# A graph-recurrent layer in three stages: one memory map, and three groups of loads and set-up work moved ahead of their stage

## The chip, the core and the metric

One core of a Trainium2 chip runs the whole program. The metric is device microseconds from one launch, and the kernel before and the kernel after are timed on the same kind of chip. The engines are named as in the profile: PE (matmul) with its weight loads PEld, DVE, ACT, POOL, and SP, which issues DMAs.

## The reference

The input is 2048 samples of 50 nodes with 32 features, the number of maskers is 2. In short:

```
adj  = relu(x.reshape(B, 1600) @ masker_param[t] + masker_bias[t])      # B x 2 x 50 x 50
adj  = adj / (adj.sum(-1) + 1e-6)
m    = adj @ (x @ weight)                                               # B x 2 x 50 x 32
gates = m @ w_ih.T + b_ih + x @ w_hh.T + b_hh ;  r, z, n                # a GRU cell
h    = (1 - z) * tanh(r * n) + z * x
h    = batchnorm over B (3200 features), then layernorm per sample
w    = softmax over nodes of (h @ attn_w + attn_b);  out = sum_n w * h  # B x 64
```

The batch statistics need h of all samples, so the last part can't start before the whole of h is there.

## The kernel before

The batch is cut into 16 tiles of 128 samples. Three stages follow each other, each in a block of its own: all engines leave a block together before any enters the next.

**Stage 1** (`stage1`, L84) makes the normalised adjacency and stores it in HBM (`adjT`). The 5000 columns are 10 groups of 500, the tiles two blocks of 8; for each block and group, eight windows, one for each tile, of 38 matmuls (L340), 160 windows in all. Both operands are split into a high and a low part by ACT and DVE (`split_x_hi`, `split_x_lo`, `split_w_hi`, `split_w_lo`). In the window that follows, ACT applies the relu (L229), DVE normalises (L276 to L284), PE transposes (L321), ACT evacuates (L235), and SP stores (L138). SP waits at the end for its last stores (L171, L172).

**Stage 2** (`stage2`, L379) first loads four small weight arrays (L455), multiplies two of them (L663), lets DVE lay the product and `whh` out in the blocks of `wd` (24 copies, L559 and L560), and splits `wd` (L471 on ACT, L565 on DVE). Then it goes through the tiles in 8 rounds each, with two buffers for the tile's data: `adj_sb` in two DMAs from `adjT` (L440), `xs_sb` (L442) and `xg_sb` (L445). A round s on PE is `aggregate(s + 1)` (L674) and then `gates(s)` (L699, L705). In round 6 of a tile the PE waits, between these two, for the next tile's `adj` and `xs` (`adj_loaded`, in `gates`). ACT splits `xg` in four parts (L486), POOL makes the low part (L652). With h of a tile ready, DVE turns it (L614), PE transposes it in seven batches of up to four chunks through one PSUM bank (L716, `turn_chunks`), ACT copies each (L498) and stores it (L505) and DVE takes statistics (L603). For the last tile these seven batches run after the rounds, with nothing beside them.

**Stage 3** (`stage3`, L737) loads 12 arrays (L839) and then h of its first block of 512 samples in 28 DMAs (L848, seven sets of three or four chunks). DVE forms mean and variance (L879 to L888), waits for all 12 arrays, and goes on from L891 to the coefficients `Csq` (L904). ACT waits for the same arrays, casts the `spread` matrix (L1035, read from the second half of `h3`, so `load_h(1)` waits for this cast), loads its table and takes the square root (L1037). With `Csq`, ACT squares the 25 chunks of a block (L1047 for PE, L1052 for POOL); POOL adds 14 of them in 13 steps (L1134), PE closes the sums (L1177), and the softmax and the pooling of the block follow. All queues are in order and the order is written out by hand; semaphores tie the engines.

Of the kernel before, what the change touches and what calls it, by code (L numbers as in the profile page):

```python
# [10 lines left out]

# [4 lines left out]
fp32 = mybir.dt.float32  # L16
# [67 lines left out]
def stage1(nc, psum, xT, W, adjT, ident_d):  # L84
    with ExitStack() as ctx:
        sb = lambda name, shape, dt=fp32: ctx.enter_context(nc.sbuf_tensor(name, shape, dt))
        sem = lambda name: ctx.enter_context(nc.semaphore(name))
        x_hi = sb("x_hi", [P, KC, BLK * P], fp32r)
        x_lo = sb("x_lo", [P, KC, BLK * P], fp32r)
# [3 lines left out]
        w_raw = sb("w_raw", [P, KC + 1, GW])  # L93
# [4 lines left out]
        at = sb("at", [RK, 2, AK, P])  # L98

# [6 lines left out]
        at_stored = [sem("at_stored0"), sem("at_stored1")]  # L106
        dve_step = sem("dve_step")

# [11 lines left out]
        def _(sp):  # L120
# [25 lines left out]
            sp.dma_start(ident[:, :], ident_d).then_inc(ident_loaded, 16)  # L146
            for blk in range(BLOCKS):
                for it, group in p1_iters(sp, blk):
                    for w in range(BLK):
# [17 lines left out]
                        if isinstance(it, int) and it == GROUPS - 1 and blk + 1 < BLOCKS:  # L167
                            load_x(BLK + w, 0)
                            load_x(BLK + w, 1)
            store_tile(ITERS * BLK - 1, 1, TILES - 1, GROUPS - 1)  # L170
            sp.wait_ge(at_stored[0], 16 * (ITERS * BLK // 2))  # L171
            sp.wait_ge(at_stored[1], 16 * (ITERS * BLK // 2))  # L172

        def split_x_hi(act, bt, half):
            act.wait_ge(x_loaded[half], 16 * (bt + 1))
            if bt >= BLK and half == 0:

                act.wait_ge(mm_done, (GROUPS - 1) * BLK + bt - BLK + 1)
            cols = bass.ts(bt % BLK, P)
            if half == 0:  # L180
                nc.scalar.copy(x_hi[:, 0:XH, cols], x_raw[:, 0:XH, :]).then_inc(x_hi_ready, 1)
            else:
                nc.scalar.copy(x_hi[:, XH:KF, cols], x_raw[:, XH:KF, :])
                nc.scalar.copy(x_hi[0:KLAST, KF, cols], x_raw[0:KLAST, KC, :])
                nc.scalar.copy(x_lo[:, KF, cols], x_raw[:, KF, :]).then_inc(x_hi_ready, 1)

        def split_x_lo(dve, bt, half):
            dve.wait_ge(x_hi_ready, 2 * bt + half + 1)
            cols = bass.ts(bt % BLK, P)
            k0, k1 = (0, XH) if half == 0 else (XH, KF)  # L190
            last = nc.vector.tensor_tensor(x_lo[:, k0:k1, cols], x_raw[:, k0:k1, :], x_hi[:, k0:k1, cols].bitcast(fp32),
                                           ALU.subtract)
            if half:
                last = nc.vector.tensor_tensor(x_lo[KR:P, KF, cols], x_raw[KR:P, KF, :], x_lo[KR:P, KF, cols].bitcast(fp32),
# [29 lines left out]
        def _(act):  # L224
# [17 lines left out]
            for blk in range(BLOCKS):  # L242
                for it, group in p1_iters(act, blk):
                    static = isinstance(it, int)
                    for w in range(BLK):
# [18 lines left out]
                        if static and it == GROUPS - 1 and w >= 1:  # L264
                            for half in range(2):
                                split_x_hi(act, BLK + w - 1, half)
            c = ITERS * BLK - 1
# [4 lines left out]
        def _(dve):  # L272
            def normalise(c, c2, start=False):
# [8 lines left out]
                if not start:  # L282
                    dve.wait_ge(tr_done, c - 1)
                nc.vector.tensor_tensor(an[:, c2], u[:, c2], rows[:, 2].unsqueeze(2).to_broadcast([P, GN, N]),  # L284
                                        ALU.mult).then_inc(an_ready, 1)

# [5 lines left out]
            for blk in range(BLOCKS):  # L292
                for it, group in p1_iters(dve, blk):
                    static = isinstance(it, int)
                    for w in range(BLK):
# [12 lines left out]
                        if static and it == GROUPS - 1 and w >= 1:  # L308
                            for half in range(2):
                                split_x_lo(dve, BLK + w - 1, half)  # L310
            normalise(ITERS * BLK - 1, 1)

        @block.tensor
        def _(pe):
# [9 lines left out]
            def window(it, w, blk, c, start=False, bank_free=False, none_before=False):  # L324
# [3 lines left out]
                cols = bass.ts(w, P)  # L328
                for i, (k0, k1) in enumerate(UNITS):
# [4 lines left out]
                    for k in range(k0, k1):  # L334
# [4 lines left out]
                        for n, (a, b, r) in enumerate(products):  # L339
                            last = nc.tensor.matmul(mm_out(w % 2), a[0:r, k, cols], b[0:r, k, :],  # L340
# [10 lines left out]
            for blk in range(BLOCKS):  # L351
                for it, group in pe_iters(pe, blk):
# [26 lines left out]
def stage2(nc, psum, ins, adjT, hF, stats):  # L379


    with ExitStack() as ctx:
        sb = lambda name, shape, dt=fp32: ctx.enter_context(nc.sbuf_tensor(name, shape, dt))
        sem = lambda name: ctx.enter_context(nc.semaphore(name))
        adj = sb("adj_sb", [2 * N, 2, TN, SH])
        xs = sb("xs_sb", [2 * N, 2, SH, 2 * D])
        xg = sb("xg_sb", [P, 2, ROUNDS, N * QB])
# [4 lines left out]
        hC = sb("hC", [P, FC, P])  # L392
        ident = sb("ident2_sb", [P, P])
        m_hi = sb("m_hi", [P, 2, RC], fp32r)
        m_lo = sb("m_lo", [P, 2, RC], fp32r)
        r_gate = sb("r_gate", [P, RC])
        n_in = sb("n_in", [P, 2, RC])
        wT4 = sb("wT4_sb", [D, P])
        wih = sb("wih_sb", [D, 3 * D])
        whh4 = sb("whh_sb", [P, 3 * D])  # L400
        biases = sb("biases_sb", [P, 2, 3])
        bias = sb("bias", [P, 3])
        wd = sb("wd", [P, 2, 2, P])
        wd_hi = sb("wd_hi", [P, 2, 2, P], fp32r)
        wd_lo = sb("wd_lo", [P, 2, 2, P], fp32r)

        consts_loaded, ident_loaded = sem("consts_loaded"), sem("ident_loaded")
        g_product, zeroed, blocks_ready = sem("g_product"), sem("zeroed"), sem("blocks_ready")
        wd_hi_ready, wd_ready, bias_ready = sem("wd_hi_ready"), sem("wd_ready"), sem("bias_ready")
        adj_loaded = [sem("adj_loaded0"), sem("adj_loaded1")]  # L410
        xg_loaded = [sem("xg_loaded0"), sem("xg_loaded1")]
# [19 lines left out]
        turn_bank = psum[:, 7 * BANK:8 * BANK]  # L431
# [5 lines left out]
        def _(sp):  # L437
            def load_adj(tile, r):
                for half in range(2):
                    sp.dma_start(adj[N * half:N * half + N, r], adjT[tile, :, SH * half:SH * half + SH].rearrange("(c m) s -> m c s", m=N)  # L440
                                 ).then_inc(adj_loaded[r], 16)
                sp.dma_start(xs[:, r], ins["xz"][tile]).then_inc(adj_loaded[r], 16)  # L442

            def load_xg(tile, r):
# [911 lines left out]
```

## Time and profile before

| what | us |
|---|---|
| median of 3 runs (2312.24 to 2316.13) | 2314.57 |
| the profiled execution's own time | 2318.24 |
| its span | 2316.5 |
| stage 1, to the last copy of the adjacency (L235) | 1463.95 |
| from there to the first aggregation of stage 2 (L674) | 38.9 |
| stage 2, to the last store of h issued (L505) | 2080.84 |
| from there to the first square of stage 3 (L1052) | 27.7 |
| mean granted clock of PE over the span, of full speed | 0.973 |

The profile is of one execution; times in it count from the start of its span. PE is busy for 2198.9 us of it (95%), DVE for 47%, ACT for 42%, POOL for 6%. Matmuls are pipelined, so a busy PE is not a PE at its peak.

### The profile page before, as it was taken

How to read it: one execution, taken by the hardware profiler on the slowest of the kernel's cores; microseconds unless marked ns; L12 is line 12 of the kernel's file. 1: busy time of each engine (PE TensorE's matmuls, PEld its weight loads, DVE VectorE, ACT ScalarE, POOL GpSimd, SP SyncE). 2: the span in 40 equal slices, each digit the busy share in tenths (PEclk: the TensorE clock that was granted, in tenths of full speed). 3: DMA queues.
4: the chain of work that ended last, by engine and by line, in shares of the span. 5: the costliest groups of instructions: out<-in, count | busy, mean ns of one | idle time of the engine just before them, and what ended most of it. 6: DMA issues, size and time to landing. Idle time of an engine off the chain costs nothing. (4 is left out here: it accounts for less than half of the span.)

```text
span 2316.5 us, 34741 instructions
## 1 busy us (share of the span) xinstructions
PE 2198.9 (95%) x12302; PEld 1737.8 (75%) x12302; DVE 1091.0 (47%) x2177; ACT 962.2 (42%) x1637; POOL 136.2 (6%) x124
## 2 busy tenths in 40 slices
PE   8999999999999999999999999299999999975888
PEld 7888888888888888888888888277777777752333
DVE  4433233332345223333233332178888888873656
ACT  4322122221234212222122221088888988865551
POOL 0000000000000000000000000011101111104340
PEclk9999999999999999999999999699999999986899
DMA  6421222212234222221222211577777677619440
GB/s 208 151 75 44 88 91 90 74 45 88 92 128 143 64 90 90 91 69 50 89 90 91 72 48 27 124 171 184 186 201 181 188 199 181 181 65 261 122 119 5
DMA packets 341744, 264.06 MB, mean 114 GB/s; under 512 B 169334, under 2 KB 302998, under 8 KB 339990
## 3 DMA queue, kind: packets, MB, share of 16 engines
q1 hardware_dynamic: 323546, 225.69, 34.5%
q10 hardware_dynamic: 18144, 37.69, 5.0%
q8 instruction: 29, 0.48, 0.1%
q14 instruction: 25, 0.20, 0.0%
HBM read 195.65 MB, written 67.70 MB: 114 GB/s over the span
## 5 line engine op out<-in xcount | busy, mean ns | idle before, releaser
L340 PE MATMUL psum<-w_hi,x_lo 128*128 128x500 f32 x2080 | 823.0, 396 | 8.6 <-DVE w_lo L216 8.6
L340 PE MATMUL psum<-w_lo,x_hi 128*128 128x500 f32 (+1 forms) x2080 | 811.0, 390 | 0.0
L340 PE MATMUL psum<-w_hi,x_hi 128*128 128x500 f32 x1920 | 745.1, 388 | 0.0
L276 DVE TENSOR_REDUCE rows<-u 128x10 f32<-128x500 f32 x160 | 107.7, 673 | 893.5 <-ACT u L229 892.8
L340 PEld LDWEIGHTS psum<-w_hi,x_lo 128*128 128x128 f32 x2080 | 392.1, 188 | 84.4 <-issue 7.9
L340 PEld LDWEIGHTS psum<-w_lo,x_hi 128*128 128x128 f32 (+1 forms) x2080 | 392.5, 189 | 73.2
L340 PEld LDWEIGHTS psum<-w_hi,x_hi 128*128 128x128 f32 x1920 | 361.7, 188 | 72.9
L235 ACT COPY at<-psum 125x512 f32<-125x512 f32 x160 | 93.8, 586 | 677.4 <-PE psum L321 677.4
L229 ACT ACTIVATE u<-psum 128x500 f32<-128x500 f32 x160 | 94.1, 588 | 342.4 <-PE psum L340 342.3
L674 PE MATMUL psum<-adj_sb,xs_sb 100*64 100x100 f32 x2048 | 200.6, 350 | 30.1 <-DMA xs_sb<-xz 30.1
L674 PEld LDWEIGHTS psum<-adj_sb,xs_sb 100*64 100x64 f32 x2048 | 144.4, 149 | 73.9 <-issue 63.7
L652 POOL TENSOR_TENSOR xg_lo<-xg_sb,xg_hi 128x400 fp32r<-128x400 f32 x64 | 67.1, 1049 | 1961.4 <-ACT xg_hi L486 1961.4
L520 ACT ACTIVATE r_gate<-psum,bias 64x400 f32<-64x400 f32 x256 | 151.2, 591 | 18.3 <-PE psum L699 15.8
L216 DVE TENSOR_TENSOR w_lo<-w_raw,w_hi 128x1000 fp32r<-128x1000 f32 x120 | 144.1, 1201 | 23.6 <-ACT w_hi L210 17.4
L210 ACT CAST w_hi<-w_raw 128x1000 fp32r<-128x1000 f32 (+1 forms) x140 | 135.6, 969 | 46.3 <-PE psum L340 45.0
L525 ACT ACTIVATE psum<-psum,bias 64x400 f32<-64x400 f32 x256 | 142.3, 556 | 12.7 <-DVE hG L595 6.9
L284 DVE TENSOR_TENSOR an<-u,rows 128x500 f32<-128x500 f32 x160 | 108.8, 680 | 6.9
L603 DVE BATCH_NORM_STATS2 stats<-hC 128x128 f32 (+1 forms) x400 | 88.7, 282 | 49.3 <-ACT hC L498 48.9
L321 PEld LDWEIGHTS psum<-ident_sb,an 128*125 128x125 f32 x640 | 94.1, 186 | 17.8 <-DVE an L284 3.2
L321 PE MATMUL psum<-ident_sb,an 128*125 128x128 f32 x640 | 96.0, 272 | 4.0 <-DVE an L284 4.0
L1013 DVE SCALAR_TENSOR_TENSOR pr<-h,nmu_sb,psum 128x512 f32<-128x512 f32 x100 | 70.5, 743 | 47.0 <-PE psum L1221 24.6
L570 DVE TENSOR_TENSOR m_lo<-psum,m_hi 128x400 fp32r<-128x400 f32 x128 | 70.6, 552 | 28.6 <-ACT m_hi L490 28.6
(160 smaller groups left out, 2284.8 us busy)
## 6 DMA issues: line engine op xcount, KB each, us to landing
w_raw<-W SPq DMA_DIRECT2D x140, 500.0 KB, 7.9
adjT<-at SPq DMA_DIRECT2D x160, 250.0 KB
adj_sb<-adjT SPq DMA_DIRECT2D x32, 1250.0 KB
xs_sb<-xz SPq DMA_DIRECT2D x16, 1600.0 KB
hF<-hC ACTq DMA_DIRECT2D x96, 256.0 KB, 6.7
h<-hF SPq DMA_DIRECT2D x64, 256.0 KB, 4.5
xg_sb<-xg ACTq DMA_DIRECT2D x14, 800.0 KB, 8.0
h<-hF SPq DMA_DIRECT2D x48, 192.0 KB, 3.7
```

Of the source, the lines that this page charges most:

```text
L210: nc.scalar.copy(w_hi[:, k0:k1, :], w_raw[:, k0:k1, :]).then_inc(w_hi_ready, 1)
L216: nc.vector.tensor_tensor(w_lo[:, k0:k1, :], w_raw[:, k0:k1, :], w_hi[:, k0:k1, :].bitcast(fp32), ALU.subtract).then_inc(w_ready, 1)
L229: nc.scalar.activation(u[:, c2].rearrange("p n m -> p (n m)"), mm_out(c2), ACT.Relu).then_inc(u_ready, 1)
L235: nc.scalar.copy(at[:, c2].rearrange("p k b -> p (k b)"), tr_out(c2)).then_inc(at_ready, 1)
L276: nc.vector.tensor_reduce(rows[:, 0], u[:, c2], AX.X, ALU.add).then_inc(dve_step, 1)
L284: nc.vector.tensor_tensor(an[:, c2], u[:, c2], rows[:, 2].unsqueeze(2).to_broadcast([P, GN, N]), ALU.mult).then_inc(an_ready, 1)
L321: last = nc.tensor.transpose(tr_out(c2)[:, k * P:(k + 1) * P], flat[:, k * RK:(k + 1) * RK], ident[:, :])
L340: last = nc.tensor.matmul(mm_out(w % 2), a[0:r, k, cols], b[0:r, k, :], start=k == 0 and n == 0, stop=k == KF and n == 1)
L520: last = nc.scalar.activation(r_gate[half], rz_bank(pair)[half], ACT.Sigmoid, bias=bias[half, R_G:R_G + 1])
L525: last = nc.scalar.activation(z_bank[half], rz_bank(pair)[other], ACT.Sigmoid, bias=bias[other, Z_G:Z_G + 1])
L603: last = nc.vector.bn_stats(stats[:, bass.ds(tile, 1), c, :].rearrange("p i v -> p (i v)"), hC[:, c, :])
L674: last = nc.tensor.matmul(out_[SH * i:SH * i + SH, :, gi], xs[:, r, b, :], adj[:, r, :, b], start=True, stop=True)
```

## The change

All of SBUF becomes one allocation, and every buffer gets a fixed place in it (`place`, `Bump`), and some buffers of a later stage share their place with buffers that the stage before has finished with. `x_hi` and `x_lo` are laid out tile by tile instead of chunk by chunk. Semaphores and buffers that two stages use are made once (`Shared`).

- In stage 1 SP loads the four small weight arrays right after its first loads; PE makes their product between the two blocks; in the last group DVE lays out `wd` (third window), ACT casts it (fourth), DVE splits it (fifth). SP loads `adj`, `xs` and `xg` of tile 0 in the last group, over `w_raw`, the first tiles of `x_hi` and of `x_lo`. The waits for the last stores move from the end of stage 1 into stage 2, behind the loads of tile 1.
- In stage 2 SP loads nine of the 12 arrays of stage 3 after the loads of tile 3, and five of the seven sets of h of the first block once tile 14's aggregations are through. The last tile's transposes alternate between two PSUM banks.
- In stage 3 `ident` is that of stage 2; SP loads the last two sets of h first, then `spread` and `pool_mask`. DVE waits for those two only before `pool_cols`. ACT loads the square root's table with a one-element activation at the start, squares two sets, and then waits for the two arrays and casts `spread`.
- h in `h3` is stored by sets (`PLACE_OF`), so that a set is one contiguous stretch.

```diff
+AT_H = 600
+AT_W_RAW, AT_X_HI = 0, (KC + 1) * GW
+AT_X_LO = AT_X_HI + BLK * KC * P
+AT_XG = AT_X_LO + 4 * KC * P
+AT_WEIGHTS = 51616
+AT_EARLY = 47768
...
+XS_TILES, XG_TILES = 3, 5
...
+def load_adj(sp, shared, adjT, tile, r=0):
+    for half in range(2):
+        sp.dma_start(shared.adj[r][N * half:N * half + N], adjT[tile, :, SH * half:SH * half + SH].rearrange("(c m) s -> m c s", m=N)
+                     ).then_inc(shared.adj_loaded[r], 16)
+def load_xs(sp, shared, ins, tile, r=0):
+    sp.dma_start(shared.xs[r][:], ins["xz"][tile]).then_inc(shared.adj_loaded[r], 16)
...
+        w_raw = place("w_raw", [P, KC + 1, GW], AT_W_RAW)
+        x_hi = place("x_hi", [P, BLK, KC, P], AT_X_HI, fp32r)
+        x_lo = place("x_lo", [P, BLK, KC, P], AT_X_LO, fp32r)
...
+            for dst, src in ((shared.wT4, "wT4"), (shared.wih, "wihT"), (shared.whh4, "whhT4"), (shared.biases, "biases")):
+                sp.dma_start(dst[:], ins[src]).then_inc(shared.weights_loaded, 16)
...
+                        if isinstance(it, int) and it == ITERS - 1:
+                            if w == 0:
+                                sp.wait_ge(w_ready, ITERS * NU)
+                                for c2 in range(2):
+                                    sp.wait_ge(at_stored[c2], 16 * (GROUPS * BLK // 2))
+                                load_adj(sp, shared, adjT, 0)
+                            if w == XS_TILES:
+                                sp.wait_ge(mm_done, it * BLK + XS_TILES)
+                                load_xs(sp, shared, ins, 0)
+                            if w == XG_TILES:
+                                sp.wait_ge(mm_done, it * BLK + XG_TILES)
+                                load_xg(sp, shared, ins, 0)
             store_tile(ITERS * BLK - 1, 1, TILES - 1, GROUPS - 1)
-            sp.wait_ge(at_stored[0], 16 * (ITERS * BLK // 2))
-            sp.wait_ge(at_stored[1], 16 * (ITERS * BLK // 2))
...
-                nc.scalar.copy(x_hi[:, 0:XH, cols], x_raw[:, 0:XH, :]).then_inc(x_hi_ready, 1)
+                nc.scalar.copy(x_hi[:, w, 0:XH, :], x_raw[:, 0:XH, :]).then_inc(x_hi_ready, 1)
...
+            def weight_blocks(dve):
+                wd = shared.wd
+                dve.wait_ge(w_ready, ITERS * NU)
+                nc.vector.memset(wd[:], 0.0).then_inc(zeroed, 1)
+                dve.wait_ge(zeroed, 1)
+                dve.wait_ge(shared.weights_loaded, 64)
+                dve.wait_ge(g_product, 1)
+                for j in range(4):
+                    q = slice(D * j, D * j + D)
+                    pair, one = divmod(j, 2)
...
+                        nc.vector.tensor_copy(wd[q, 0, of, first:first + D], g_bank[q, e])
+                        last = nc.vector.tensor_copy(wd[q, 1, of, first:first + D], shared.whh4[q, e])
+                last.then_inc(blocks_ready, 1)
+                nc.vector.tensor_tensor(shared.bias[:], shared.biases[:, 0], shared.biases[:, 1], ALU.add).then_inc(shared.bias_ready, 1)
...
+                        if static and it == ITERS - 1 and w == 2:
+                            weight_blocks(dve)
+                        if static and it == ITERS - 1 and w == 4:
+                            dve.wait_ge(wd_hi_ready, 1)
+                            nc.vector.tensor_tensor(shared.wd_lo[:], shared.wd[:], shared.wd_hi[:].bitcast(fp32),
+                                                    ALU.subtract).then_inc(shared.wd_ready, 1)
...
+                if blk == 1:
+                    pe.wait_ge(shared.weights_loaded, 64)
+                    nc.tensor.matmul(g_bank, shared.wT4[:], shared.wih[:], start=True, stop=True).then_inc(g_product, 1)
...
+SETS = [(n, list(range(n, FC, QC))) for n in range(QC)]
+SET_AT = [sum(len(cs) for _, cs in SETS[:n]) for n in range(QC)]
+PLACE_OF = {c: SET_AT[n] + j for n, cs in SETS for j, c in enumerate(cs)}
+EARLY_SETS = 5
+A_SLOT = TN * SH + SH * 2 * D
+assert EARLY_SETS < QC and SET_AT[EARLY_SETS] * CW <= A_SLOT
+def load_set(sp, shared, hF, i, n):
+    at = slice(SET_AT[n], SET_AT[n] + len(SETS[n][1]))
+    for k in range(CB):
+        sp.dma_start(shared.h[:, i % 2, at, k * P:(k + 1) * P], hF[i * CB + k, :, slice(n, FC, QC), :]).then_inc(shared.h_loaded[i % 2][n], 16)
...
-        turn_bank = psum[:, 7 * BANK:8 * BANK]
...
+        def turn_bank(tile, n):
+            bank = 0 if isinstance(tile, int) and tile == TILES - 1 and n % 2 else 7
+            return psum[:, bank * BANK:(bank + 1) * BANK]
...
+                        load_adj(sp, shared, adjT, tile + 2, r)
+                        load_xs(sp, shared, ins, tile + 2, r)
             sp.dma_start(ident[:], ins["ident"]).then_inc(ident_loaded, 16)
-            load_xg(1, 1)
-            load_adj(1, 1)
+            load_xg(sp, shared, ins, 1, 1)
+            load_adj(sp, shared, adjT, 1, 1)
+            load_xs(sp, shared, ins, 1, 1)
+            for c2 in range(2):
+                sp.wait_ge(shared.at_stored[c2], 16 * (ITERS * BLK // 2))
             iteration(0, True)
+            for dst, src in early_loads(shared, ins):
+                sp.dma_start(dst, src).then_inc(shared.early_loaded, 16)
             with sp.Fori(1, TILES // 2 - 1) as it:
                 iteration(it, True)
-            iteration(TILES // 2 - 1, False)
+            sp.wait_ge(ax_done, (TILES - 1) * ROUNDS)
+            for n in range(len(batches)):
+                sp.wait_ge(hC_stored[n], 16 * CB)
+            for n in range(EARLY_SETS):
+                load_set(sp, shared, hF, 0, n)
...
+                wait(pe, hC_ready, tile * len(batches) + (n - 1 if isinstance(tile, int) and tile == TILES - 1 and n else n))
...
+def early_loads(shared, ins):
+    return [(shared.quarter[:], ins["quarter"]), (shared.score_mask[:], ins["score_mask"]),
+            (shared.square_mask[:], ins["square_mask"]), (shared.fold_out[:], ins["fold_out"]), (shared.par[:], ins["par"]),
+            (shared.aw[:], ins["aw"]), (shared.ab[:], ins["attn_b"].partition_broadcast(P)),
+            (shared.rowpar[:], ins["rowpar"]), (shared.t_mask[:], ins["t_mask"])]
...
-        loads = [(ident[:], ins["ident"]), (quarter[:], ins["quarter"]),
-                 (score_mask[:], ins["score_mask"]), (square_mask[:], ins["square_mask"]),
-                 (pool_mask[:], ins["pool_mask"]), (spread_raw, ins["spread"]), (fold_out[:], ins["fold_out"]),
-                 (par[:], ins["par"]), (aw[:], ins["aw"]), (ab[:], ins["attn_b"].partition_broadcast(P)),
-                 (rowpar[:], ins["rowpar"]), (t_mask[:], ins["t_mask"])]
+        loads = [(spread_raw, ins["spread"]), (pool_mask[:], ins["pool_mask"])]
         @block.sync
         def _(sp):
-            for dst, src in loads:
...
+            def load_h(i, first=0):
+                for n in range(first, QC):
...
+                        sp.wait_ge(pr_ready, FC * (i - 2) + 1 + max(order.index(c) for c in SETS[n][1]))
+                    load_set(sp, shared, hF, i, n)
...
-            load_h(0)
+            load_h(0, EARLY_SETS)
+            for dst, src in loads:
+                sp.dma_start(dst, src).then_inc(loaded, 16)
...
-            dve.wait_ge(loaded, 16 * len(loads))
+            dve.wait_ge(shared.early_loaded, 16 * len(early_loads(shared, ins)))
...
+            dve.wait_ge(loaded, 16 * len(loads))
...
-            act.wait_ge(loaded, 16 * len(loads))
-            nc.scalar.copy(spread[:].rearrange("p c f -> p (c f)"), spread_raw).then_inc(spread_ready, 1)
+            act.wait_ge(step_done, 2)
+            nc.scalar.activation(warm[:], eps[:], ACT.Sqrt)
...
-            squares(0, *range(QC))
+            squares(0, 0, 1)
+            act.wait_ge(loaded, 16 * len(loads))
+            nc.scalar.copy(spread[:].rearrange("p c f -> p (c f)"), spread_raw).then_inc(spread_ready, 1)
+            squares(0, *range(2, QC))
```

## Rows read from the trace of the kernel before

**Rows 1.** Busy tenths of PE in 40 slices of 57.9 us, from the page

```profile
PE   8999999999999999999999999299999999975888
```

**Rows 2.** Timeline around the first boundary: start, us, engine, line, operation, idle before

```profile
1459.66 0.39 PE L340 MATMUL psum<-w_lo,x_hi 97*128 97x500 f32 x1
...
1460.72 0.67 DVE L276 TENSOR_REDUCE rows<-u 128x10 f32<-128x500 f32 x1 [7.19 <-ACT u L229]
...
1463.36 0.59 ACT L235 COPY at<-psum 125x512 f32<-125x512 f32 x1 [2.67 <-PE psum L321]
1468.84 0.36 SPq L455 DMA_DIRECT2D wT_sb<-wT  x1
...
1471.12 10.27 SPq L440 DMA_DIRECT2D adj_sb<-adjT  x2
...
1471.97 0.74 PE L663 MATMUL psum<-wih_sb,wT_sb 32*128 32x96 f32 x2 [8.65 <-DMA biases_sb<-biases]
...
1490.60 21.07 SPq L440 DMA_DIRECT2D adj_sb<-adjT  x2
...
1502.84 2.98 PE L674 MATMUL psum<-adj_sb,xs_sb 100*64 100x100 f32 x32 [30.13 <-DMA xs_sb<-xz]
...
1505.80 0.70 PE L699 MATMUL psum<-m_hi,wd_lo 64*128 64x400 f32 x2
```

**Rows 3.** Timeline of DVE, ACT and SP at the end of the second stage

```profile
2071.46 0.83 DVE L603 BATCH_NORM_STATS2 stats<-hC 128x6 f32<-128x128 f32 x4
...
2071.91 0.59 ACT L498 COPY hC<-psum 128x512 f32<-128x512 f32 x1 [1.27 <-PE psum L716]
...
2080.84 0.34 ACTq L505 DMA_DIRECT2D hF<-hC  x1
...
2082.84 0.37 SPq L839 DMA_DIRECT2D ident_sb<-ident  x1
```

**Rows 4.** Timeline of DVE, ACT, POOL and PE at the head of the third stage

```profile
2089.42 0.99 DVE L888 TENSOR_REDUCE var_sb<-pr 128x25 f32<-128x800 f32 x1
...
2102.04 2.86 ACT L1035 CAST spread_sb<-h 100x3200 fp32r<-100x3200 f32 x1 [21.23 <-DMA t_mask_sb<-t_mask]
2104.91 1.28 ACT L1037 ACT_TABLE_LOAD   x1
...
2106.62 0.32 DVE L896 RECIPROCAL inv_sb<-bnstd_sb 128x25 f32<-128x25 f32 x1 [3.67 <-ACT bnstd_sb L1037]
...
2108.54 1.52 ACT L1052 ACTIVATE sqp<-h,Csq_sb,A_sb 128x512 f32<-128x512 f32 x2 [2.02 <-DVE Csq_sb L904]
...
2120.23 9.78 POOL L1134 TENSOR_TENSOR acc<-acc,sqp 128x512 f32<-128x512 f32 x7 [2.36 <-ACT sqp L1052]
...
2131.97 1.04 PE L1177 MATMUL psum<-acc,square_mask_sb 128*32 128x512 f32 x2 [2.27 <-POOL mark L1137]
```

**Rows 5.** Groups by line: busy us, mean ns, idle before

```profile
L486 ACT CAST xg_hi<-xg_sb 128x400 fp32r<-128x400 f32 x64 | 33.6, 529 | 0.0
...
L559 DVE COPY wd<-psum 32x32 f32<-32x32 f32 x12 | 2.2, 182 | 3.4 <-PE psum L663 3.3
```

**Rows 6.** Timeline of PE around the seventh round of the first tile

```profile
1531.35 0.45 PE L699 MATMUL psum<-m_hi,wd_lo 64*128 64x400 f32 x2
```

**Rows 7.** Stretches: busy time of PE, PEld, DVE, ACT, POOL, granted clock, DMA share, GB/s

```profile
1471.00:1529.00 58.00, 26.90 (x218) 21.47 (x219) 18.36 (x52) 21.69 (x41) 5.64 (x6) 0.68 0.75 175
1529.00:1532.00 3.00, 3.00 (x28) 2.37 (x28) 1.83 (x4) 2.86 (x7) 0.51 (x1) 1.00 0.05 11
2020.00:2040.00 20.00, 20.00 (x174) 15.74 (x174) 16.85 (x39) 17.51 (x35) 2.18 (x3) 1.00 0.09 32
```

**Rows 8.** Waits of the SP queue over the whole span

```profile
SPq L440 <- PE psum L674: 231.0, 14, 17.9
```

**Rows 9.** Stretches at the head of the third stage, columns as in rows 7

```profile
2094.00:2102.00 8.00, 0.00 (x0) 0.00 (x0) 0.00 (x0) 0.00 (x0) 0.00 (x0) 0.50 0.65 143
2104.00:2116.00 12.00, 7.44 (x38) 6.12 (x42) 8.79 (x19) 9.65 (x13) 5.36 (x4) 0.50 1.16 292
```

More of the change, by code:

```diff
@@ L12 @@
+import math
 import concourse.bass as bass
 from concourse import mybir
+from collections import namedtuple
 from contextlib import ExitStack
@@ L266, in _ @@
                                 split_x_hi(act, BLK + w - 1, half)
+                        if static and it == ITERS - 1 and w == 3:
+                            act.wait_ge(blocks_ready, 1)
+                            nc.scalar.copy(shared.wd_hi[:], shared.wd[:]).then_inc(wd_hi_ready, 1)
             c = ITERS * BLK - 1
@@ L285, in normalise @@
                                         ALU.mult).then_inc(an_ready, 1)
+            def weight_blocks(dve):
[8 more added lines that the diff above has]
+                    pair, one = divmod(j, 2)
+                    at = {R_G: SH * pair + D * one, Z_G: SH - SH * pair + D * one, N_G: D * j}
+                    for gate, first in at.items():
+                        of, e = (N_W if gate == N_G else RZ_W), slice(D * gate, D * gate + D)
+                        nc.vector.tensor_copy(wd[q, 0, of, first:first + D], g_bank[q, e])
+                        last = nc.vector.tensor_copy(wd[q, 1, of, first:first + D], shared.whh4[q, e])
+                last.then_inc(blocks_ready, 1)
+                nc.vector.tensor_tensor(shared.bias[:], shared.biases[:, 0], shared.biases[:, 1], ALU.add).then_inc(shared.bias_ready, 1)
             split_x_lo(dve, 0, 0)
@@ L437, in _ @@
         def _(sp):
[L438 to L444, printed above, removed]
-                sp.dma_start(xg[:, r], ins["xg"][tile]).then_inc(xg_loaded[r], 16)
             def iteration(it, more):
@@ L548, in _ @@
         def _(dve):
-            nc.vector.memset(wd[:], 0.0).then_inc(zeroed, 1)
-            dve.wait_ge(zeroed, 1)
-            dve.wait_ge(consts_loaded, 64)
-            dve.wait_ge(g_product, 1)
-            for j in range(4):
-                q = slice(D * j, D * j + D)
-                pair, one = divmod(j, 2)
-                at = {R_G: SH * pair + D * one, Z_G: SH - SH * pair + D * one, N_G: D * j}
-                for gate, first in at.items():
-                    of, e = (N_W if gate == N_G else RZ_W), slice(D * gate, D * gate + D)
-                    nc.vector.tensor_copy(wd[q, 0, of, first:first + D], psum[q, e])
-                    last = nc.vector.tensor_copy(wd[q, 1, of, first:first + D], whh4[q, e])
-            last.then_inc(blocks_ready, 1)
-            nc.vector.tensor_tensor(bias[:], biases[:, 0], biases[:, 1], ALU.add).then_inc(bias_ready, 1)
-            dve.wait_ge(wd_hi_ready, 1)
-            nc.vector.tensor_tensor(wd_lo[:], wd[:], wd_hi[:].bitcast(fp32), ALU.subtract).then_inc(wd_ready, 1)
             dve.wait_ge(bias_ready, 1)
@@ L661, in _ @@
         def _(pe):
-            pe.wait_ge(consts_loaded, 64)
-            nc.tensor.matmul(psum[:, 0:3 * D], wT4[:], wih[:], start=True, stop=True).then_inc(g_product, 1)
             pe.wait_ge(wd_ready, 1)
@@ L673, in aggregate @@
                         b = 32 * i + q * QB + gi
-                        last = nc.tensor.matmul(out_[SH * i:SH * i + SH, :, gi], xs[:, r, b, :], adj[:, r, :, b], start=True, stop=True)
+                        last = nc.tensor.matmul(out_[SH * i:SH * i + SH, :, gi], xs[r][:, b, :], adj[r][:, :, b], start=True, stop=True)
                 last.then_inc(ax_done, 1)
```

170 lines of the change are left out of this document (88 added, 82 removed).

## The prediction

> **What bounds the kernel now.** I read the page's busy line first, then the two places where it dips. PE is at 8 tenths or more from the start to slice 37 of 40, except in slice 26 (2 tenths) and in slices 36 to 40 [rows 1]. So PE sets the time of stages 1 and 2, and stage 3 is a chain over all engines. The change adds no work inside the loops; what it can give back lies at the two dips. The timeline of the first dip: the last matmul of stage 1 starts at 1459.66, the last copy of the adjacency ends at 1463.36 + 0.59 = 1463.95, SP gets to stage 2 only at 1468.84, and PE starts its first aggregation at 1502.84, after 30.13 us of waiting for a DMA [rows 2]. The weight product at 1471.97 and all that DVE does with it is over long before; the loads alone end this wait. The second dip: the last store of h is issued at 2080.84, stage 3 opens at 2082.84 [rows 3], DVE has the variance at 2089.42 + 0.99 = 2090.41, yet ACT gets its arrays only at 2102.04, casts `spread` (2.86), loads a table (1.28), and DVE's reciprocal comes at 2106.62 and the first square at 2108.54 [rows 4]. The last seven batches of transposes before it go at 1.27 + 0.59 = 1.86 us each, PE and ACT taking turns over one bank [rows 3].
>
> **The first boundary.** Loads of tile 0 move into the last group, the wait for the last stores moves behind the loads of tile 1. After 1463.95 remain the issue of one store (0.34 to 0.36 [rows 2, 3]) and the change of blocks. I put that change at 0.8: its bounds are 0 and 2.0, the whole of the way from the last store to the next stage's first DMA at the other boundary, landing included [rows 3]. PE then aggregates from 1465.1 on: 1502.84 - 1465.1 = **37.7 gained** (36.5 to 38.5). From aggregation to first gate it was 2.96 us (1502.84 to 1505.80 [rows 2]). ACT now has the four casts of `xg` there, 4 x 0.53 = 2.1 us [rows 5], which formerly lay beside the DMA wait; with the casts of m behind them, on ACT and DVE, the gate comes at about 3 again. I count 0, between 0 and 1.
>
> The cover in the last group. DVE sat idle 7.19 us before it took up the window's work [rows 2]; 24 copies at 182 ns apiece would be 4.4 us even if none overlapped [rows 5], so they fit in one window, and so do the casts. Uncovered, that would be 4 us, once. SP issues two `adj` DMAs in 10.27 us [rows 2], a little over one window, so the store queued behind them is late by about 1 us, and lands behind them. The evacuation that needs this store's buffer is two windows, 18 us, later, so I count 0. The four small arrays at the start add four issues of about 0.4 us ahead of the load of tile 1, whose data queue behind the first W loads anyway: 0. The product on PE, now between two matmul streams, costs up to its own 0.74 [rows 2]; I take 0.3, since half of that row was a PE at half clock: **0.3 lost**.
>
> What is late next. Tile 1's data are wanted in round 6 of tile 0, at 1531.35 before [rows 6], that is 28.5 us after the first aggregation. Before, SP had issued tile 1's `adj` from 1490.60 on [rows 2] while PE still waited; now these loads start only with the block, at 1465.1. The two tiles' loads together ran from 1471 to about 1529 without a hole at 175 GB/s, and then the queue was empty (11 GB/s) [rows 7]. So one tile takes about 58 / 2 = 29 us and a little for issue and landing: it lands at about 1465.3 + 29 + 1.5 = 1495.8, and PE asks at 1531.35 - 37.7 = 1493.7. **2 lost** to a new wait for `adj_loaded` in round 6. Bounds: 0, if it goes like the second tile (1502.84 to 1529, 26.2); 4, if like the first (1471.12 to 1502.84, 31.7). Behind it on PE stand the gates of round 6 and everything after, so it is all on the path. SP's wait for the last stores stands behind these loads, and the next load there is for tile 2, 28 us on. Tile 2 starts and is wanted later by the same 2, so it isn't late again; SP idles 231.0 / 14 = 16.5 us before each pair of `adj` loads [rows 8], which also covers the issue of nine arrays for stage 3 at 0.4 us apiece and somewhat more for the odd-shaped ones, under 8 in all.
>
> PE's clock: in both kernels the rounds begin after low activity, so I take no change. If the first round ran at 2.4 instead of 1.2 GHz, it would be worth about half of such a stretch of matmuls, some 1.2 by the 28.5 / 7 = 4.1 us of a round; the low bound takes it in.
>
> First boundary: -37.7 + 0.3 + 2.0 = **-35.4** (-38.9 to -33).
>
> **The second boundary.** The five early sets of h are 16 transfers of 256 KB and 4 of 192 KB, 5 MB, 17 us at the 292 GB/s of such loads [rows 9]. They start near 2026, eight rounds of some 4.4 us before the last gates, when the DMAs are busy 9% of the time [rows 7], and land before 2050. Four terms follow.
> - Transposes in two banks: ACT then paces them, 0.59 for a copy and 0.34 for the store's issue, 0.97 with gaps instead of 1.86 [rows 3]; over the five full turns that is 4.45, and some 0.2 in the short last. DVE follows: four statistics in 0.83 from 2071.46 [rows 3], 25 by 2077, so ACT's last store, at 2076.2, ends the stage. **-4.6** (0 to -5).
> - DVE has no array to wait for after the variance: 2102.04 - 2090.41 go [rows 4]. **-11.6**.
> - The cast and the table are out of the way of the root. DVE waited 3.67 for it [rows 4]; now the root (0.3) runs beside DVE's next four small steps (0.9). **-3.7**. The chain from there to `Csq` (1.9) stays. First square: 2108.54 - 19.9.
> - New: ACT squares eight chunks (8 x 0.71 = 5.7) and then waits for `spread` and `pool_mask`. Stage 3 opens at 2078.2; data flow 1.3 later; the two last sets, 1.57 MB, at 292 GB/s take 5.4. For `spread`, 1.28 MB, I take the 143 GB/s of 2094 to 2102, when it held the queue [rows 9]: 9.0. `pool_mask` adds 1.5: landed at about 2095.5 to 2096. ACT is ready at 2088.6 + 5.7 = 2094.3. The cast itself (2.86) mostly fills a pause: POOL waited 2.36 for ACT in this place, before 2120.23, and from there its chain of eight additions runs up to PE's closing matmul at 2131.97 [rows 4]. So the cast costs about 0.5, and each us that ACT waits for it costs one: 1.7 here, with 0.3 for the hand-over. **+2.5** (0.5, if all goes at 292 GB/s; 6.5, if all that the 12 arrays took over 4.4 us is `spread`'s).
>
> Second boundary: -4.6 - 11.6 - 3.7 + 2.5 = **-17.4** (-20 to -13). After the first block's sums the stage is as before: h of block 1 starts loading after the cast, at about 2099, with an empty queue, and is wanted from 2115 on.
>
> Two rules of the Trainium skill bear on these terms. The 143 GB/s go with a DMA share of 0.65, against 1.16 at 292 GB/s [rows 9]. The Trainium skill's page "DMA: Bandwidth & Descriptors", section on why a DMA increments its semaphore by 16, says that a transfer over 100 partitions is spread over 10 of the 16 engines; `spread` has 100 rows, so the slow rate would be its own and not its neighbours'. By that rule the last term is 2.5, by plain bytes 0.5. Against the third term stands the Trainium skill's page "ScalarE: Activation LUTs", section "What ACT_TABLE_LOAD costs": a switch costs 1.28 us and a drain of 1.38 more. By it the table moved away would be worth 1.4 more. The trace shows the root starting right behind the 1.28, so the row decides.
>
> **Sum.** -35.4 - 17.4 = -52.8. The profiled execution took 2318.24 (span 2316.5), which would become 2265.4. It is 3.7 above the median of the runs shown, 2314.57; none of the terms depends on that, so the median becomes **2261.8**.
>
> **Rivals.**
> - *No new waits* (20%). Tile 1 goes at the second tile's pace, `spread` at full rate: -37.4 - 19.4 = -56.8, 2257.8. For it: tile 1 is alone in the queues. Against: half-idle DMA engines in [rows 9].
> - *The transfers take back more* (18%). Tile 1 like the first tile, `spread` at its slow end, and the last transposes gain 2.4 less: -33.4 - 11.0 = -44.4, 2270. For it: the queue is the limit in both places. Against: before, both also carried neighbours.
> - *Stage 1 pays for the preload* (5%). Stores of the last group queue behind `adj` in the same queue. An `adj` load over 23 us (18 us of two windows and 5 more) holds the evacuation, then PE. Tile loads of 29 us, half of it `adj`, speak against it. At twice that length it costs 6 a load, some 12 in all: 2274.
> - *Slower* (4%). Every operand moves in SBUF, and `x_hi` and `x_lo` change layout. If PE's reads suffer, it is in the 160 x 38 = 6080 matmuls of stage 1. It decides from 52.8 / 6080 = 8.7 ns each on, 3.6% of the 1459.66 / 6080 = 240 ns that one takes, its share of the transposes included [rows 2]. At 12 ns it is +73 - 53: 2335. Against: each row read is 128 or 500 contiguous words in both.
> - *The change doesn't do what it says*: SP reaches the early loads late, because its waits come in the order written. A preload that only starts with stage 2 gives 4 instead of 37.7: 2295 (1%).
>
> Forecast 52%. What lies between 2254 and 2272 holds eight in ten: it leaves out part of the third case and the last three. A change of under 0.2% (4.6 us) couldn't be told from none: faster by more 95%, the same 1%, slower 4%.
>
> **What would show it.** PE's first aggregation 1 to 2 us after the last copy of stage 1; a wait of 0 to 4 us of PE for a DMA in round 6 of tile 0 and in no later tile; the last copies of h one us apart; the first square 12 us after the last store of h instead of 27.7; a wait of 1 to 3 us of ACT before the cast of `spread`, after eight squares; POOL's first chain as long as before. More than 242 ns for each matmul of stage 1, a hole in its last group, or waits for `adj` in later tiles would prove it wrong.

## The result: slower by 7 us, and the profile after

The changed kernel took 2321.97 us in the median (2317.26 to 2326.76, 9 runs), the kernel before 2314.63 beside it (9 runs): a ratio of 1.0035, interval 1.0024 to 1.0047. I had forecast 2261.8 and 95% for faster. The profiled execution took 2321.97, its span 2320.2.

The page of the kernel after, PE's busy tenths [rows 1]: slice 26 is at 7 instead of 2, and slices 28, 30 and 34 behind it are at 8, where PE had been at 9 throughout.

```profile
PE   8999999999999999999999999798989998996888
```

The first boundary, in the timeline of the kernel after (start, us, engine, line, operation, idle before) [rows 2]:

```profile
1460.89 0.59 ACT L302 COPY at<-psum 125x512 f32<-125x512 f32 x1 [2.67 <-PE psum L416]
1462.26 0.36 SPq L549 DMA_DIRECT2D ident_sb<-ident  x1
...
1462.45 1.58 PE L753 MATMUL psum<-adj_sb,xs_sb 100*64 100x100 f32 x16 [1.59 <-PEq L136]
...
1467.30 1.62 PE L753 MATMUL psum<-adj_sb,xs_sb 100*64 100x100 f32 x16 [3.27 <-DMA ident_sb<-ident]
...
1501.58 0.70 PE L778 MATMUL psum<-m_hi,wd_lo 64*128 64x400 f32 x2 [6.31 <-issue]
```

PE aggregates 1.0 us after the last copy, as forecast. The second aggregation then waits for `ident`, which I hadn't seen, and round 6 waits 6.3 for tile 1, where I had 2. The view puts this wait down to "issue"; it is the one for tile 1's loads, for it is gone in the last experiment below, where these loads come earlier.

The second boundary, same view [rows 3, 4]:

```profile
2096.05 0.59 ACT L596 COPY hC<-psum 128x512 f32<-128x512 f32 x1 [0.49 <-ACT hC L596]
...
2097.13 0.59 ACT L596 COPY hC<-psum 128x512 f32<-128x512 f32 x1 [0.49 <-PE psum L795]
...
2099.57 0.34 ACTq L603 DMA_DIRECT2D hF<-hC  x1
...
2111.98 1.52 ACT L1128 ACTIVATE sqp<-h,Csq_sb,A_sb 128x512 f32<-128x512 f32 x2 [2.47 <-DVE Csq_sb L979]
...
2138.63 1.91 PE L1256 MATMUL psum<-acc,square_mask_sb 128*32 128x512 f32 x2 [2.23 <-POOL mark L1216]
```

Copies 1.08 apart, the first square 12.4 us after the last store instead of 27.7: this is the forecast. What the forecast doesn't have lies between the boundaries. The waits of the kernel after over the whole span (total us, times, longest) [rows 8]:

```profile
PE psum L778 <- DMA xs_sb<-xz: 29.5, 8, 5.5
...
SPq L120 <- PE psum L753: 138.3, 12, 16.0
```

PE, which before waited for tile loads only once, now waits for them in the middle of the stage, and SP idles 11.5 us before a pair of `adj` loads instead of 16.5. A stretch of steady tiles, of the kernel after and then of the kernel before (columns as in rows 7):

```profile
1700.00:2030.00 330.00, 313.21 (x2575) 249.58 (x2573) 265.24 (x593) 269.88 (x510) 34.53 (x33) 0.96 0.80 172
```

```profile
1700.00:2030.00 330.00, 329.98 (x2796) 261.50 (x2796) 286.19 (x651) 293.59 (x558) 41.19 (x40) 1.00 0.70 186
```

The DMA engines are busier (0.80 for 0.70) and move less (172 for 186 GB/s): each byte costs them more. PE's granted clock is 0.96 instead of 1.00. One wait, as PE and SP have it in the kernel after:

```profile
1812.06 11.56 SPq L120 DMA_DIRECT2D adj_sb<-adjT  x2
1823.80 16.31 SPq L126 DMA_DIRECT2D xs_sb<-xz  x1
```

```profile
1852.38 0.70 PE L778 MATMUL psum<-m_hi,wd_lo 64*128 64x400 f32 x2 [5.47 <-DMA xs_sb<-xz]
1852.85 0.56 PE L778 MATMUL psum<-m_lo,wd_hi 64*128 64x400 f32 x2
...
1859.56 0.34 PE L778 MATMUL psum<-m_lo,wd_hi 64*128 64x400 f32 x2
```

SP is held 28 us by the three issues of tile 10, and PE goes on at 1852.4, 40 us after the first. A tile took 35.1 us of PE, so that is 5 too many.

The wait costs more than its own length. Behind it PE's granted clock is 0.50 (1.2 GHz) up to 1858, and 1.00 (2.4 GHz) again from 1859 on; the same pair of matmuls takes 0.56 us at the lower clock and 0.34 at the higher. Over the twelve steady tiles of the table below PE is idle for 31.8 us (before: none) and busy for 434.6 instead of 421.3 for the same work, at a mean granted clock of 0.95 instead of 1.00. So of the 45.1 us lost there 31.8 are waits and 13.4 are the clock behind them.

Where the time went, by five marks that both kernels have (last matmul of stage 1; SP's first `adj` issue for tiles 3 and 15; last store of h; closing matmul of block 0; end). "On 256" is the experiment below that removes the cause, in its second run:

| stretch | before | after | on 256 |
|---|---|---|---|
| to the last matmul of stage 1 | 1459.7 | 1457.2 (-2.5) | 1456.3 (-3.4) |
| to tile 3's load | 106.4 | 81.1 (-25.2) | 76.0 (-30.4) |
| twelve steady tiles | 421.3 | 466.4 (**+45.1**) | 421.6 (+0.3) |
| to the last store of h | 93.5 | 94.8 (+1.3) | 89.8 (-3.7) |
| to block 0's closing matmul | 51.1 | 39.1 (-12.1) | 39.1 (-12.0) |
| to the end of the span | 184.5 | 181.6 (-3.0) | 183.7 (-0.8) |

Some of this is the run and not the change. Six runs of the kernel before with spare words alone have the last matmul at 1457.1 to 1458.5, where the profiled one has it at 1459.7. They take 47.1 to 50.3 from the last store to the closing matmul, where it takes 51.1. In all traces, whatever the kernel, the last stretch lies between 181.6 and 187.9, and two traces of the kernel on 256 alone have 187.8 and 183.7.

### The profile page after: what moved, and what is told of

Same layout as the page of the kernel before. It is cut to its first block and busy times, and to the rows that moved or that the text cites. A ratio compares the mean times of both kernels' runs of the same rounds, so it can differ in the third digit from the quotient of the medians.

```text
span 2320.2 us, 34746 instructions
## 1 busy us (share of the span) xinstructions
PE 2210.4 (95%) x12302; PEld 1749.6 (75%) x12302; DVE 1089.8 (47%) x2177; ACT 963.3 (42%) x1638; POOL 135.4 (6%) x124
## 5 line engine op out<-in xcount | busy, mean ns | idle before, releaser
L277 ACT CAST w_hi<-w_raw 128x1000 fp32r<-128x1000 f32 (+1 forms) x140 | 135.7, 969 | 46.4 <-PE psum L434 45.1
L661 DVE SCALAR_TENSOR_TENSOR n_in<-psum,bias,r_gate 128x400 f32<-128x400 f32 x128 | 79.9, 625 | 73.4 <-PE psum L784 71.7
L684 DVE BATCH_NORM_STATS2 stats<-hC 128x128 f32 (+1 forms) x400 | 88.5, 281 | 36.3 <-ACT hC L596 35.6
L778 PE MATMUL psum<-m_hi,wd_lo 64*128 64x400 f32 x256 | 60.1, 465 | 42.1 <-DMA xs_sb<-xz 29.5
```

Of the source, the lines that this page charges most:

```text
L277: nc.scalar.copy(w_hi[:, k0:k1, :], w_raw[:, k0:k1, :]).then_inc(w_hi_ready, 1)
L684: last = nc.vector.bn_stats(stats[:, bass.ds(tile, 1), c, :].rearrange("p i v -> p (i v)"), hC[:, c, :])
```

## Experiments

**The suspicion.** The one map of memory moved the tile buffers. Before, `adj_sb` stood at byte 26112 of a partition, a multiple of 256, as did `xs_sb`, `xg_sb` and `hC`; after, the map's base is 16512 and `AT_H` adds 2400, so that all of them stand 224 bytes past one. (The traces hold no addresses: 16512 is where free memory starts in the program as built, and 26112 is that and the 9600 bytes of `stats` ahead of `adj_sb`. That 256 bytes more change nothing below, and 32 do, bears it out.) `adj_sb` is filled in runs of 256 bytes: 32 loads of 1250 KB would be 160000 of them, and the page counts 169334 packets under 512 bytes before. Theory A: a place off a multiple of 256 makes these loads dearer. Rival B: the pairs are late because tile 1 was late and never catch up. Rival C: what lies beside them in the new map matters.

**On multiples of 256.** The kernel after, with one edit:

```
-            base = -(-nc.sbuf_base // 32) * 32
+            base = -(-nc.sbuf_base // 32) * 32 + 32
```

> The kernel after with its whole arena moved up by 32 bytes: adj, xs, xg and h then begin at multiples of 512 bytes, as adj, xs and xg did in the kernel before; in the kernel after they begin 224 bytes behind a multiple of 256. Theory A (the tile loads of stage 2 are slow because their destinations begin off a 64- or 256-byte boundary): no PE wait for xs from the third tile on, rounds back to 35.7 us a tile, xs issues back from 14 to about 8.7 us, and 2262 us (2256 to 2270), the forecast. Rival B (the new schedule: the first loads of stage 2 start with PE already at work and the queue never catches up): unchanged, 2322. Rival C (the new places in SBUF share something with what the engines read and write at the time): unchanged, 2322, since 32 bytes move nothing to another region.

Measured: 2266.7 us (4 runs), 0.9796 of before (0.978 to 0.9812). Run again later: 2268.26 (5 runs), 0.9808 (0.9794 to 0.9823). 32 bytes are worth some 54 us. PE's waits for `xs_sb` are gone, and SP idles 211.2 / 13 = 16.2 us before a pair again (waits of the second run).

**The kernel before, moved.** If A holds, the old kernel must get slower by spare words alone, ahead of its `adj_sb`; by B and C it can't. Three sizes, 32, 64 and 256 bytes:

```
+        pad = sb("pad2", [P, 8])     # 16 and 64 in the other two
         adj = sb("adj_sb", [2 * N, 2, TN, SH])
```

> The kernel before with 32 unused bytes per partition ahead of the buffers of stage 2, so that adj, xs and xg begin 32 bytes behind a multiple of 256. Schedule and regions are those of before. Theory A: tiles take 40 us or more instead of 35.7, so 14 tiles lose 4 to 6 us each: 2370 to 2400. Rivals B and C: 2315.

> The same with 64 bytes: aligned to 64, not to 256. If the unit that counts is 64 bytes or less: 2315. If it is 256 bytes (each adj packet is one 256-byte run, which then spans two units): as slow as with 32 bytes, 2370 or more. Rivals B and C: 2315.

> Control: the same with 256 bytes. Theory A in each of its forms up to 256: 2315, like the kernel before. If 512 bytes were the unit (adj then begins at 256 mod 512), slower, 2340 or more. If it is the moving itself that costs (rival C): anything but 2315.

Measured, one run each: 2384.2, 2342.0 and 2313.57, against 2314.59 for before (7 runs). The waits of the one with 32 bytes:

```profile
PE psum L700 <- DMA xs_sb<-xz: 29.2, 7, 6.4
```

The old kernel shows the new one's waits, with no edit of its order or neighbours. A stands; B and C fall as causes of the loss. And 32 costs more than 64, which neither of my two expectations for 64 bytes had (2315, or 2370 and more).

**Which buffer.** The waits name `xs_sb`, but it is the last of three loads in one queue. So `adj_sb` alone by 32 bytes, then `xs_sb` alone:

```
+        pad2 = sb("pad2", [P, 8])
         adj = sb("adj_sb", [2 * N, 2, TN, SH])
+        pad2b = sb("pad2b", [P, 56])
```

> Kernel before with adj_sb alone moved by 32 bytes (8 spare words a partition ahead of it, 56 behind it, so that xs_sb, xg_sb and hC keep a multiple of 256). Theory A1, the price is one more piece for each run of 256 bytes of a packet, so that short packets pay most (adj_sb is filled by packets of 256 bytes, xs_sb by long ones): nearly all of the loss of the run with everything shifted comes back here, 2370 to 2385 us, PE waiting some 25 us or more for the pair of loads, SP's wait before a pair near 160 us in 14. Theory A2, the price goes by bytes, whatever the packet: adj is 61% of a pair's 4.1 MB, the pair's load grows by 6 us instead of 10 and the time is near 2335 to 2345, as with a shift by 64. Theory C, adj's place costs nothing and xs_sb's is what counts (the late landings were named xs): 2313 to 2317.

> Kernel before with xs_sb alone moved by 32 bytes (8 spare words ahead of it, 56 behind it). Theory A1 (a price for each packet, xs_sb's being long): 2313 to 2318 us, no wait of PE for xs_sb. Theory A2 (a price by bytes): the pair's load grows by about 4 us, which fits into most of the slack before round 6, so 2316 to 2325. Theory C (xs_sb alone counts): 2370 or more.

Measured: 2376.27 (4 runs), 1.0272 (1.0255 to 1.0289), and 2315.16 (10 runs), 1.0001 (0.999 to 1.0011). It is `adj_sb` alone, with its short runs; `xs_sb`, 16 KB on end in a partition, costs nothing 32 bytes off. The waits with `adj_sb` alone moved still say `xs_sb`:

```profile
PE psum L701 <- DMA xs_sb<-xz: 28.8, 10, 5.4
```

The wait is for three DMAs and is put down to the last of them. The name is that of the victim.

**How far off.** The same words as in the first move, 32 of them, 128 bytes:

> Kernel before with everything behind x_lo in stage 2 moved by 128 bytes. If what counts is a boundary at every 256 bytes (a run of 256 bytes is cut in two, wherever): slower as with 64, 2335 to 2350, SP's wait near 170 us in 14. If 128 bytes is enough: 2313 to 2317 and waits of SP near 230 us.

Measured: 2352.36 (4 runs), 1.018 (1.0161 to 1.02). A half of 256 isn't enough. The table has means over the loads of tiles 3 to 15. "SP held" is from the SP timelines, from the start of the first of a tile's three issues to the end of the last. The packets are the DMA packets that the traces hold with their times, over the twelve steady tiles: those of 256 bytes fill `adj_sb`. And "landed" is the end of the last packet of `xs_sb`, counted from the start of the first issue.

| `adj_sb` past a multiple of 256 | runs | SP held, us | one 256-byte packet, ns | landed, us | a tile, us |
|---|---|---|---|---|---|
| 0 | before, pad of 256, `xs_sb` alone, after on 256 | 17.9 to 18.3 | 19.9 to 20.1 | 31.2 to 31.3 | 35.1 |
| 64 or 128 | pads of 64 and 128 | 24.0, 24.1 | 25.5, 25.0 | 35.9, 36.1 | 36.5, 36.8 |
| 32 or 224 | pad of 32, `adj_sb` alone, after | 27.0 to 27.3 | 27.4 to 28.6 | 39.4 to 39.8 | 38.1 to 38.9 |

Three levels: 64 or 128 bytes off costs a pair 6 us of SP, 32 or 224 bytes off costs 9. It is the short packets that become dearer: those of 16 KB, of `xs_sb`, take 838 ns in the kernel before and 813 to 901 in the moved ones. The column "landed" tells when PE must wait: at 31 us a tile of 35.1 has 4 to spare, at 36 and at 40 it has nothing.

The Trainium skill's page "DMA: Bandwidth & Descriptors", section "How a descriptor splits into AXI transactions", says that a descriptor is cut into transactions of 256 bytes, and that one which doesn't start at a multiple of 256 has its first transaction start at the multiple below; it says so of reads. By it, as an estimate, a run of 256 bytes off a multiple takes two transactions instead of one, and a run of 16 KB 65 instead of 64. The runs here agree for writes into SBUF in that the short runs pay and the long ones don't. That 32 and 224 bytes cost more than 64 and 128 doesn't follow from it, and no run here shows why.

**What was left of the forecast.** On 256 the change brings 45 to 48 us instead of 53 (2266.7 against 2314.59, 2268.26 against 2313.08). The first thing missing is the wait for `ident`. In this run the wait stands ahead of the first transposes that need `ident`, and its load is issued behind those of tile 1:

```
             aggregate(0)
-            pe.wait_ge(ident_loaded, 16)
             turn(0, True)
...
+                if isinstance(it, int) and it == 0 and r and q == 1:
+                    pe.wait_ge(ident_loaded, 16)
```

> Kernel after on multiples of 256, and PE's wait for ident put ahead of the first transposes (round 1 of tile 1) instead of behind the first aggregation; the load of ident is issued behind adj and xs of tile 1. The run on multiples of 256 had PE waiting 2.8 us for ident behind the first aggregation and about 3 us in round 6 of tile 0 for tile 1's pair, each at a clock held by nothing else. If both are on the end's path: 2266.7 - 2.8 = 2263.9, less up to 0.3 since the pair leaves one issue earlier. If the time gained at the first aggregation is only given to the wait in round 6 (the pair lands when it lands): 2266.7, with that wait near 6 us. I expect the second for the most part: 2265.5 to 2267.

Measured: 2270.19 (4 runs), 0.9818 (0.9801 to 0.9834): no gain. PE's waits from 1459 to 1530, first on 256, then with `ident` moved:

```profile
PE psum L753 <- DMA ident_sb<-ident: 2.8, 1, 2.8
...
PE psum L778 <- issue: 1.8, 1, 1.8
```

```profile
PE psum L778 <- issue: 4.6, 1, 4.6
```

2.8 + 1.8 has become 4.6, and PE goes on at 1495.1 with `ident` moved and at 1494.9 without: the pair of tile 1 lands when it lands. The two waits are one, and the trace had shown it as two.

**Masks earlier.** On top of that, `spread` and `pool_mask` are issued ahead of the two last sets of h:

```
+            for dst, src in loads:
+                sp.dma_start(dst, src).then_inc(loaded, 16)
             load_h(0, EARLY_SETS)
-            for dst, src in loads:
-                sp.dma_start(dst, src).then_inc(loaded, 16)
```

> As the run before it, and at the second boundary spread and pool_mask are issued ahead of the two sets of h that stage 3 waits for instead of behind them. ACT waited 2.24 us for pool_mask ahead of the cast. If the sets still come in time (the first squares of sets 5 and 6 come some 10 us behind the opening of stage 3): 1.5 to 2.2 us less than the run before it, 2263.5 to 2265. If the last two sets are now what ACT or DVE waits for: no change or up to 2 us more.

> The same kernel as the earlier run with ident and masks moved, beside the two others of this call on one chip: 2266 to 2269, and within 2 us of the kernel with the shift alone, since the wait for ident came back in round 6 and pool_mask's 2.2 us are what is left.

> The same kernel as the earlier run on multiples of 256: 2266 to 2270. If moving ident and the masks was worth their waits, it is 2 to 5 us above the run with both moved; if they came back, within 2 us of it.

Measured: 2268.49 (4 runs), 0.9807 (0.979 to 0.9823), above the 2263.5 to 2265 that I expected; again, 2264.89 (5 runs), 0.9792 (0.9779 to 0.9806), beside 2268.26 for the kernel on 256 alone. That is 1.7 us below the run with `ident` moved and 3.4 below the kernel on 256; the intervals overlap, so a gain isn't settled. The timelines of ACT, on 256 and with the masks moved, show the wait go:

```profile
2064.59 2.86 ACT L1185 CAST spread_sb<-h 100x3200 fp32r<-100x3200 f32 x1 [2.77 <-DMA pool_mask_sb<-pool_mask]
```

```profile
2061.18 2.84 ACT L1186 CAST spread_sb<-h 100x3200 fp32r<-100x3200 f32 x1
```

From the last store to block 0's closing matmul it is 36.3 in both traces with the masks moved, and 38.6 to 39.1 in the three on 256 without. From there to the end it is 185.4 and 186.8 with, and 187.8, 183.7 and 186.1 without: a spread of 4 us between traces of one kernel, in which a gain or loss of 2.5 can't be seen.

**All of tile 1 ahead.** On top of that again: PE's 5 us in round 6 go if tile 1's loads start in the last group too. They need free places: `x_hi` of the fourth tile goes to the last of the eight places and those of the tiles behind it move down by one, and `adj` of tile 1 lies over that last place and `x_lo` of the first four tiles.

```
+ADJ1_TILES, XS1_TILES = 4, 6
+X_POS = (0, 1, 2, 7, 3, 4, 5, 6)
...
+                            if w == ADJ1_TILES:
+                                sp.wait_ge(mm_done, it * BLK + ADJ1_TILES)
+                                load_adj(sp, shared, adjT, 1, 1)
```

> As the run with ident and masks moved, and the loads of tile 1 (adj, xs, xg) are issued in the last group of stage 1 too, behind tiles 4 and 6 of it, into places that are free by then (x_hi of tile 3 changes place with that of tile 7, adj of tile 1 lies over it and x_lo of tiles 0 to 3; all on multiples of 256 still but the group's total of bytes rises by 4.9 MB). PE waited 5.6 us for tile 1's pair in round 6 of tile 0. If that wait goes and nothing of stage 1 waits: 5.6 us less than the run before, about 2261 to 2263, and 2260 to 2264 with the spread of the runs. If the last group of stage 1 is now bound by its queue (stores of adjT stand behind 9.8 MB of loads on SP's queue): up to 8 us of it come back as holes of PE in the last group or a later first aggregation, 2268 to 2271.

Measured: 2264.26 (5 runs), 0.9791 (0.9777 to 0.9804), the same as its neighbour's 2264.89, just above the first of my two ranges (2260 to 2264). The wait in round 6 is gone. In its place, at the boundary:

```profile
1453.34 13.28 SPq L195 DMA_DIRECT2D adjT<-at  x2
...
1459.35 0.59 ACT L311 COPY at<-psum 125x512 f32<-125x512 f32 x1 [2.85 <-PE psum L425]
...
1467.31 3.00 PE L759 MATMUL psum<-adj_sb,xs_sb 100*64 100x100 f32 x32 [7.99 <-PEq L138]
```

SP is still held by the last stores when ACT has made its last copy, and every engine waits at the end of the block for SP: PE starts at 1467.3 instead of 1461.0. It is the later first aggregation that my second case for this run named, and it takes what the wait of 5.5 us in round 6 gave. This and the kernel with the masks moved are 2.1% faster than the kernel before, the lowest medians that ran, though their intervals overlap with that of the kernel on 256 alone.

## Why the prediction was wrong

**The step that failed** is the one that put the steady tiles at nothing: "Tile 2 starts and is wanted later by the same 2, so it isn't late again; SP idles 231.0 / 14 = 16.5 us before each pair". It took the duration of a tile's load from the trace of before and let it stand, though the change gives each of its buffers another address. 16.5 us of SP's idleness looked like ample cover. But SP's issues end well before the data are in: before, they held SP for 18 us, and the data had landed after 31. Of a tile's 35.1 us that left 4, and not 16.5, and the loads of the kernel after take 40. Twelve steady tiles cost 45.1 us (31.8 of waits and 13.4 of the lower clock behind them), more than the 41.5 that all other stretches together brought. The prediction had named the sign, waits for `adj` in later tiles, and no rival with this mechanism.

**The slower rival had the right object and the wrong reader.** "Every operand moves in SBUF" was priced for PE's reads in stage 1. These didn't change: 394, 390 and 387 ns for the three kinds of matmul against 396, 390 and 388. The DMAs write there too, and here it was they that the address mattered to. I gave the case 4%. That its 2335 lies nearer to 2322 than the forecast does is luck: its mechanism didn't occur, and the one that did had no price.

**The first boundary**, -35.4 forecast, was -30.4 on 256. PE's start was right (1.0 us after the copy; I had 1.1). The product and the copies behind it left no hole. The wait in round 6 was right in kind; with the wait for `ident` ahead of it, it was 2.8 + 1.8 = 4.6 in place of 2.0. `ident` was a step I moved and didn't follow: the diff leaves PE's wait behind the first aggregation, while its load is now issued only when the block opens. The kernel after, with the loads dear, had only -25.2: it lost 5 more, since tile 1's `adj` took SP 15.3 instead of 13.7 and tile 2's load was dear too.

**The last group.** ACT waited 7.4 us for a store that stood behind the `adj` load, in the place I named, 2.1 more than in the windows around it, and PE lost nothing, as I counted. I had put the bound for this at a load of 23 us; SP was held for 14.5. On 256 it is 11.7, and ACT waits for no store. Twice the load there, in the last experiment, and the price was paid, at the end of the block instead of in the evacuation.

**The second boundary** was right within 2 us against the profiled run of before: from tile 15's load to the closing matmul -15.7 on 256, against -17.4. In part this is luck. The 27.7 us from the last store to the first square that I started from are the longest of seven traces of the old order; the other six have 24.1 to 26.9, and against the shortest the gain would be 3.6 smaller. Transposes -3.7 (4.6 forecast: copies stand 1.07 apart, I had 0.97), array wait, cast and table with the new wait -12.0 (-12.8 forecast). The first square came 12.4 after the last store, 15.3 sooner, as forecast; the new term was 3.3 instead of 2.5, with a wait of ACT of 2.77 (I had 1.7 of the 2.5 for it). The root started 0.03 us behind the variance and DVE waited for it no more, so the 3.67 of the row are gone, and nothing beyond them.

**The range**, 2254 to 2272, was made from the terms that I had listed, and for these it was wide enough: on 256 the medians are 2266.7 and 2268.3. It held nothing for a term that wasn't on the list. (Its upper end is a little tight even so: the bounds named for the first boundary add up to -36.5 + 0.3 + 4.0 = -32.2, and not -33.)

## What to carry over

When a change moves buffers, print the start address of every DMA destination before and after, modulo 256, and weigh first those with short runs: a shift that changes no instruction made the kernel before up to 3% slower. Measure the slack of a load from its first issue to its landing, and not by how long the issuing queue idles; and where it is used up, count the lower clock behind each wait too. A change that looks like a small loss may be a large gain and a larger accident; the steady stretch, where the change did nothing, is where to look, and DMA engines busier at fewer GB/s were the sign here. Before crediting a removed wait, ask what sets the next one: two waits in a row on one queue of loads can be one wait.

## What the runs showed that I had not expected

- Place in SBUF: `adj_sb` off a multiple of 256 bytes holds SP 24 us a pair (64 or 128 bytes off) or 27 (32 or 224) instead of 18, and its 256-byte packets take 25 and 27 to 29 ns instead of 20; `xs_sb`, in runs of 16 KB, costs nothing 32 bytes off (2315.16 against 2314.22).
- The length of an issue's row on SP is not the time to landing: 18 us against 31 in the kernel before, 27 against 40 in the kernel after.
- The price goes up once the slack is gone: landing at 36 us costs 1.4 to 1.7 us a tile of 35.1, landing at 39 to 40 costs 3.0 to 3.8.
- A wait of 5.5 us left PE at a granted clock of 0.50 for the 6 us behind it; in the steady tiles this is 13.4 of 45.1 us lost.
